# Experts' outputs stored to their rows in two transfers a group, and weight loads held until they are stored

## What is computed

```
dispatch, combine = softmax of x . phi over the tokens, over the slots
xs = dispatch' x                                # a row of 192 for each image and expert
y  = gelu(xs @ w1[e] + b1[e]) @ w2[e] + b2[e]   # weights of its own for each expert
h  = h + combine y                              # back to 1568 tokens
```

## Time and profile before

| what | us |
|---|---|
| median of 3 runs | 1515.61 (1510.67 to 1516.45) |
| the profiled execution, its own time | 1509.02 |
| its span, first to last instruction | 1507.3 |
| experts' stage, first store issued to mixing | 703 to 884 |
| TensorE busy | 1323.9 (88% of the span) |
| granted TensorE clock, mean | 0.952 |

### The profile page before, as it was taken

How to read it: one execution, slowest core, us unless ns; L and a number is a source line. 1 busy time by engine, 2 the same in 40 slices (tenths; PEclk the granted TensorE clock), 3 DMA queues, 4 the chain that set the end, 5 groups by cost and what they waited for, 6 DMA issues and landing times.

```text
span 1507.3 us, 18440 instructions
## 1 busy us (share of the span) xinstructions
PE 1323.9 (88%) x6684; PEld 767.2 (51%) x6684; DVE 915.8 (61%) x1513; ACT 670.9 (45%) x1206; POOL 554.6 (37%) x399
## 2 busy tenths in 40 slices
PE   7979989898989867469988859979999999999998
PEld 6634445454545434244433445547856659445444
DVE  3789999999999999972100148855446624221022
ACT  4786767677777744042110117631552241313311
POOL 1478898988989887300000020012034302000000
PEclk9999999999999999769999969999999999999999
DMA  6405051422414040344999940000010001030101
GB/s 205 172 2 172 12 162 37 135 75 98 127 46 171 12 160 0 138 178 189 395 397 396 372 103 0 1 0 1 1 38 1 2 1 31 7 110 13 37 0 33
DMA packets 38773, 151.96 MB, mean 101 GB/s; under 512 B 10364, under 2 KB 14587, under 8 KB 33948
## 3 DMA queue, kind: packets, MB, share of 16 engines
q1 hardware_dynamic: 34588, 149.21, 27.6%
q10 hardware_dynamic: 4096, 1.58, 0.4%
HBM read 147.56 MB, written 1.63 MB: 99 GB/s over the span
## 4 chain that ended last, share of the span: by engine, by line
PE 54%; DVE 20%; issue 10%; ACT 6%; DMA 5%; POOL 4%; SPq 1%; ACTq 0%; DVEq 0%; POOLq 0%
PE ps L1876 52%; DVE arena L1474 7%; DVE arena L1463 5%; DMA arena<-in_e_b 4%; POOL arena L821 3%; ACT arena L923 2%; ACT ps L1034 1%; DVE stats L1371 1%; DVE arena L1759 1%; PE ps L1885 1%; ACT arena L928 1%; DVE arena L1483 1%; SPq L633 1%; DVE arena L1763 0%; DVE arena L1514 0%
## 5 line engine op out<-in xcount | busy, mean ns | idle before, releaser
L1876 PE MATMUL ps<-arena 128*32 128x192 f32 (+17 forms) x5236 | 946.4, 415 | 97.8 <-DVE arena L1524 22.2
L1876 PEld LDWEIGHTS ps<-arena 128*32 128x32 f32 (+15 forms) x5236 | 539.7, 154 | 475.7 <-issue 277.1
L821 POOL TENSOR_TENSOR arena<-arena 128x784 f32<-128x784 f32 x192 | 368.9, 1935 | 94.0 <-DVE arena L1474 93.4
L1876 PE MATMUL ps<-arena,ident 128*128 128x392 f32 x900 | 349.3, 517 | 48.3 <-POOL arena L821 40.0
L1474 DVE TENSOR_TENSOR_SCAN arena<-ps,arena 128x784 f32<-128x784 f32 x192 | 341.0, 1777 | 2.5 <-ACT ps L1034 2.5
L1876 PEld LDWEIGHTS ps<-arena,ident 128*128 128x128 f32 x900 | 169.6, 196 | 196.5 <-POOL arena L821 70.5
L1034 ACT ACTIVATE ps<-arena 128x384 f32<-128x384 f32 x384 | 207.9, 575 | 114.2 <-DVE arena L1474 113.4
L923 ACT ACTIVATE arena<-ps 128x392 f32<-128x392 f32 (+9 forms) x265 | 124.3, 487 | 294.7 <-PE ps L1876 206.2
L923 ACT ACTIVATE arena<-ps,arena 128x392 f32<-128x392 f32 (+2 forms) x191 | 103.4, 602 | 224.5 <-PE ps L1876 139.1
L1463 DVE TENSOR_TENSOR arena<-ps,arena 128x784 f32<-128x784 f32 x192 | 182.8, 953 | 8.0 <-ACT ps L1060 6.8
L1622 DVE COPY arena<-ps 128x384 f32<-128x384 f32 x32 | 16.3, 552 | 150.7 <-PE ps L2124 150.7
(11 more groups left out here) (201 smaller groups left out, 861.0 us busy)
## 6 DMA issues: line engine op xcount, KB each, us to landing
arena<-in_e_w SPq DMA_DIRECT2D x32, 2304.0 KB
arena<-bc_rows SPq DMA_DIRECT2D x128, 392.0 KB, 4.8
arena<-in_patches SPq DMA_DIRECT2D x4, 1176.0 KB, 7.5
arena<-comb_rows SPq DMA_DIRECT2D x1, 3136.0 KB, 10.7
arena<-in_mlp_w SPq DMA_DIRECT2D x5, 576.0 KB, 4.6
arena<-arena ACTq DMA_DIRECT2D x128, 12.0 KB, 8.6
arena<-in_mlp_w SPq DMA_DIRECT2D x5, 384.0 KB, 3.6
arena<-in_mlp_w SPq DMA_DIRECT2D x10, 192.0 KB, 4.0
```

What stands on the lines that cost most here:

```text
L821: pool.tensor_tensor(pair(hbuf[:, at % SLOTS, :]), pair(hbuf[:, at % SLOTS, :]), c_all[:, n:n + 2, :], ALU.mult).then_inc(times_c, 1)
L1876: return pe.matmul(dst, lhsT, rhs, start=first, stop=last)
```

## The change

Three edits. A group's outputs are stored in two transfers, one for each parity, in place of eight: each takes 64 partitions of `ys` (every second one) to four partitions of `ysN`, 48 KB. The counts that ACT and PE wait for follow. And SP waits, behind the 11 loads of "rw", until all stores of all groups have landed, before it issues "rwB" and what follows.

```diff
@@ -723,6 +723,8 @@
                 load("rw", wu[:, 2 * j:2 * j + 1], a[name][0:128, :])
                 load("rw", wu[0:64, 2 * j + 1:2 * j + 2], a[name][128:D, :])
                 load("rw", wu[64:128, 2 * j + 1:2 * j + 2], a[name][128:D, :])
+            for k in range(2):
+                sp.wait_ge(ys_stored[k], 16 * 2 * NG // 2)
             load("rwB", w_oA, a["w_o"][0:128, :])
             load("rwB", w_oB[0:64], a["w_o"][128:D, :])
             load("rwB", w_oB[64:128], a["w_o"][128:D, :])
@@ -1162,14 +1164,14 @@
             def expert_out(g):
 
                 if g >= 2:
-                    act.wait_ge(ys_stored[g % 2], 16 * 8 * (g // 2))
+                    act.wait_ge(ys_stored[g % 2], 16 * 2 * (g // 2))
                 copy_out(s_y2, g, ys[:, g % 2, :], bank(s_y2.banks[g][0], 128, 0, D))
                 s_y2.wait_taken(act, g)
-                for j in range(EG):
-                    for par in range(2):
-                        e = par * NE + EG * g + j
-                        act.dma_start(ysN[e:e + 1, :, :], ys[32 * j + par:32 * j + 32:2, g % 2, :])\
-                            .then_inc(ys_stored[g % 2], 16)
+                for par in range(2):
+                    e = par * NE + EG * g
+                    act.dma_start(ysN[e:e + EG, :, :],
+                                  ys[par:128:2, g % 2, :])\
+                        .then_inc(ys_stored[g % 2], 16)
 
             for g in range(NG + 1):
                 if g >= 2:
@@ -2150,7 +2152,7 @@
                 if 1 <= g <= NG:
                     expert_turn(g - 1)
             for k in range(2):
-                pe.wait_ge(ys_stored[k], 16 * 8 * NG // 2)
+                pe.wait_ge(ys_stored[k], 16 * 2 * NG // 2)
             for i in range(8):
                 s_cT.wait_taken(pe, i // 2)
                 s_mix.fill(pe, i)
```

## The result

The changed kernel takes 1519.76 us (median of 20 runs, 1516.12 to 1525.99) against 1515.72 for the kernel before (20 runs, 1510.08 to 1519.98): a ratio of 1.0032, with a 95% interval of 1.0021 to 1.0043. By the ratio it is 4.9 us slower (the two medians are 4.0 us apart), less than the 7.6 us that I called a difference. The direction was forecast, the size was not: +4.9 against +10. The profiled execution took 1519.91 us (span 1518.2), 10.9 more than the one before; single executions of either kernel differ by 5 us and more, so sums are made inside the experts' stage.

A forecast was written before the change was run, and what follows sets the result against it. The experts' weights on the DMA engines, 99 to 100% busy from 703 to 866, set the pace. Last output 16 us later, with 5.7 saved behind it, gave +10: 1515.6 + 10 = 1525.6 us, range 1509 to 1545.

The forecast's parts named there:

- Part 1: ACT's issues, two in place of eight: 3.9 us less a group, a gain only in the last group.
- Part 2: End of the stage, last stores landing on empty engines: 878.0 in place of 883.69, 5.7 us saved.
- Part 3: Loads held behind SP's wait ("rwB", "tb", first MLP's weights) still land before their use: cost 0.
- Part 4, engines: Each new store, 64 rows to four partitions, goes to four engines; a group's two are 34 packets on each.
- Part 4, turns: While weights flow, ACT's queue gets one packet through per weight row, 0.80 us each: 34 packets take 27 us.
- The walk: Experts' stage, group by group: ACT's copies wait for stores, weights pause in three gaps (18 us), last output 16 us later.
- rival (a): Four engines, several rows a turn: no gaps, only 10 us of work on those engines; +4, 1520; chance 0.22.
- main case: Four engines, one packet a turn, weights pausing in the experts' stage: +10 us, 1525.6; chance 0.56.

The follow-up runs named there:

- every third group: Two stores on four engines for groups 1, 4, 7, 10, 13 and 15, eight stores for the others, with SP's wait, against the kernel before: ratio 0.9990, 1510.46 us.
- the one that was to take the waits away: The changed kernel with a ys buffer for each of the 16 groups, measured against the kernel before: 1517.43 us, ratio 1.0029.
- two engines: Four stores a group, each of 32 rows to two partitions of ysN, with SP's wait, against the kernel before: 1538.71 us, ratio 1.0159.

## Why the prediction was wrong, point by point

- **Part 1** held: 1.14 us of issue for the last group, 4.0 fewer, where 3.9 were forecast, and no gain while weights flow.
- **Part 2** held: 5.2 us won against 5.7 (3.5 of them come with the wait alone). It took the issues and the company of other loads as two savings; without SP's wait the two-store form saves nothing, the end grows to 11.7 us.
- **Part 3** held: mixing to transposes 11.5 us against 11.8.
- **Part 4, engines**: four, 68 packets a store. The rule of the Trainium skill ("Why a DMA increments its semaphore by 16 and not by 1", in DMA: Bandwidth & Descriptors) is borne out for unequal sides as well, 64 against 4, 32 against 2 and 128 against 8.
- **Part 4, turns**: one packet for one, as said: 17 and 16 packets on four engines between 788 and 791. The Trainium skill, under "Queues, rings and completion order" in DMA: Bandwidth & Descriptors, would have an engine drain a whole run of descriptors before it changes queue; these rows disagree. But the turn was mis-sized: 18.9 us / 34 = 0.56 us, where I took 0.80 from landings of stores on all sixteen engines. On the four engines of the bias rows 8 weight rows come with 3 short packets, and they are turns too. A group's stores so took 18.9 us and not 27.
- **The walk is the step that failed**, in two terms. With its turn of 0.80 us it put 18 us into three pauses of all the weights. They stood still for 7.6 us in the trace: group 2's copy was not late at all (727.42, forecast 735), group 3's came at 742.55 and not at 762. And it put the longer work of the four engines at nothing, though rival (a) had priced it at 10 us, on the condition that several rows pass in a turn. It is a cost without that condition, and without a standstill: every third group lost 3.3 us up to PE's last output, and its weights never stood still. That term belonged into the main case. 16 us were expected up to the last output, 11.8 came: one term too large and one left out in part made up for each other. With the 5.2 won that is +6.6 in the profiles and +4.9 by the ratio. That 1520 was named for (a) is luck in part: its price was about right, its mechanism was not.
- **Open**: how the loss divides, 14.1 us up to PE's last output and 11.8 after the clock gave 2.3 back. The work on four engines is 11 us by the price of (a), and an estimate of 10 scaled up from the 3.3 of every third group. That leaves, as an estimate, 3 to 4 us for the waits and for PE's half clock behind them. No run shows them apart: the one that was to take the waits away moved them into the issue.

## What to carry to other kernels

Fewer and larger transfers can be spread over fewer DMA engines: count the completions of a transfer in the profile (they are its engines), and where another stream keeps all engines busy, price a transfer by the work on the engines that carry it, since the stream went here at the pace of the slowest. Use the large form where the queue is empty and its issue is on the path, here in the last group alone, and keep other loads off the engines until it has landed. Of a long wait for a transfer ask what it holds up: 68 us of them left the weights moving in one run, and in the changed kernel one of 17.6 us ended in a stretch of 3.8 us without weights.

## What was not expected of the hardware

- Two DMA issues on ACT's queue took 7.65 to 21.07 us, against 1.15, when several groups' stores were waiting in it; with two engines, four issues took up to 20.4 us against 2.2.
- A completion or a short bias row in one queue gives the other queue a turn, as a row of 18 KB does: without the bias loads ACT's 34 packets took 22.7 us in place of 18.9.
- Beside small rows, 34 packets on four engines are no quicker than 16 on sixteen: with the later loads in flight the end took 11.6 and 11.7 us, against 10.4 with eight stores.
